# Second attention of a macaron block: the softmax sums over pre-added key halves, and a later order of the steps around them

## The reference

```
x = x + 0.5 * moe(norm(x));  x = x + attention0(norm(x));  x = x + 0.5 * moe(norm(x))
x = x + 0.5 * zones(norm(x)); x = x + attention1(norm(x));  x = x + 0.5 * zones(norm(x))
```

```
c_q, c_kv = h @ W_DQ + b_DQ, h @ W_DKV + b_DKV          # 32 features each
q = [c_q @ W_UQ + b_UQ, c_q @ W_QR + b_QR]              # 128 + 32 per head
k = [c_kv @ W_UK + b_UK, h @ W_KR + b_KR (all heads)]
attn = softmax(q k^T / sqrt(160))                       # 256 x 256 per head and batch
out = (attn @ (c_kv @ W_UV + b_UV)) @ W_O + b_O
```

## Time and profile before

| what | us |
|---|---|
| median of 3 runs | 1517.97 |
| lowest and highest | 1517.54, 1518.09 |
| the profiled execution | 1523.39 |
| its span | 1521.4 |
| TensorE busy | 1457.4 (96%) |
| VectorE busy | 1099.7 (72%) |
| ScalarE busy | 958.2 (63%) |
| GpSimd busy | 581.7 (38%) |

### The profile page before, as it was taken

One profiled execution on the slowest core, in us unless ns is written; L12 is line 12 of the kernel. 1 busy time (PEld: TensorE's weight loads), 2 busy tenths in 40 slices (PEclk: granted clock), 3 DMA queues, 4 the chain that ended last, 5 costly groups with the idle time before them and its releaser, 6 DMA issues.

```text
span 1521.4 us, 27946 instructions
## 1 busy us (share of the span) xinstructions
PE 1457.4 (96%) x9950; PEld 1186.2 (78%) x9950; DVE 1099.7 (72%) x2377; ACT 958.2 (63%) x1710; POOL 581.7 (38%) x551
## 2 busy tenths in 40 slices
PE   6999999889999999999999999999979999989998
PEld 6788888775666665688888877899967777769998
DVE  3766766688888888476667665577768888866765
ACT  6455555447777777655555554777736666668886
POOL 4466566510000000026666653677710111136664
PEclk9999999999999999999999996999999999999999
DMA  6000000000000000000000003000000000000000
GB/s 176 1 1 1 1 0 2 1 0 2 1 1 1 1 2 1 1 1 1 2 0 1 1 26 143 1 2 2 2 1 2 1 2 2 2 2 2 15 15 29
DMA packets 13320, 16.88 MB, mean 11 GB/s; under 512 B 768, under 2 KB 10496, under 8 KB 12928
## 3 DMA queue, kind: packets, MB, share of 16 engines
q1 hardware_dynamic: 13184, 15.11, 3.2%
HBM read 13.01 MB, written 2.10 MB: 10 GB/s over the span
## 4 chain that ended last, share of the span: by engine, by line
PE 84%; DVE 8%; ACT 4%; issue 2%; DMA 1%; POOL 0%; DVEq 0%; SPq 0%; POOLq 0%; ACTq 0%
PE PS L604 20%; PE PS L632 10%; PE PS L1748 9%; PE PS L1761 8%; PE PS L741 5%; PE PS L761 5%; PE PS L749 4%; PE PS L1118 2%; PE PS L718 2%; PE PS L1093 2%; PE PS L1122 2%; PE PS L170 2%; PE PS L1075 1%; PE PS L1103 1%; PE PS L1142 1%
## 5 line engine op out<-in xcount | busy, mean ns | idle before, releaser
L542 POOL TENSOR_TENSOR RR<-AR,RR 128x512 fp32r<-128x512 f32 x150 | 193.9, 1293 | 490.7 <-ACT RR L565 490.7
L579 ACT ACTIVATE AR<-PS 128x512 f32<-128x512 f32 x224 | 134.0, 598 | 197.2 <-PE PS L604 196.0
L521 DVE TENSOR_TENSOR AR<-AR,PS 128x512 f32<-128x512 f32 x224 | 153.8, 687 | 132.3 <-PE PS L604 132.2
L859 ACT ACTIVATE AR<-PS 128x512 f32<-128x512 f32 x256 | 152.3, 603 | 85.9 <-PE PS L749 85.2
L932 DVE TENSOR_REDUCE AR<-PS 128x2 f32<-128x512 f32 x256 | 172.3, 686 | 21.5 <-PE PS L741 20.8
L604 PE MATMUL PS<-XHI,WG 128*128 128x512 f32 x448 | 175.7, 392 | 0.0
L604 PE MATMUL PS<-XHI,WU 128*128 128x512 f32 x448 | 174.6, 390 | 0.2
L525 DVE TENSOR_TENSOR AR<-AR,PS 128x512 f32<-128x512 f32 x224 | 153.9, 687 | 7.9 <-POOL RR L542 0.3
L1748 PE MATMUL PS<-XHI,SL 128*128 128x256 f32 x576 | 133.7, 287 | 2.6 <-DVE XTR L1914 1.5
L1748 PE MATMUL PS<-XLO,SL 128*128 128x256 f32 x576 | 133.0, 286 | 1.5 <-DVE XTR L1914 1.3
L741 PE MATMUL PS<-XLO,XHI 128*128 128x512 f32 x256 | 129.5, 506 | 3.0 <-DVE AR L932 2.4
(11 more groups left out here) (299 smaller groups left out, 3489.4 us busy)
## 6 DMA issues: line engine op xcount, KB each, us to landing
X<-in_x SPq DMA_DIRECT2D x4, 512.0 KB, 6.6
RAWZ<-in_zone_up SPq DMA_DIRECT2D x8, 256.0 KB, 5.0
RAWZ<-in_zone_down SPq DMA_DIRECT2D x8, 256.0 KB, 5.6
out_x<-X SPq DMA_DIRECT2D x4, 512.0 KB, 3.2
AR<-in_w SPq DMA_DIRECT2D x1, 1792.0 KB, 11.7
XT<-in_w SPq DMA_DIRECT2D x1, 1608.0 KB, 8.8
XT<-in_sel SPq DMA_DIRECT2D x1, 896.0 KB, 6.8
SM<-in_small SPq DMA_DIRECT2D x1, 857.5 KB, 7.2
```

The lines of the kernel that those rows point to most:

```text
L521: v.tensor_tensor(PRD[:, m % 2, :], SIL[:, m % 2, :], bank(2 + m % 2), ALU.mult).then_inc(S.prod, 1)
L542: g.tensor_tensor(HL[k % 3], GAT[:, m % 2, :], HH[k % 3].bitcast(F32), ALU.subtract).then_inc(S.h_lo, 1)
L579: act.activation(SIL[:, m % 2, :], bank(m % 2), ACT.Silu).then_inc(S.silu, 1)
L859: act.activation(PT[:, g % 2, k, 2 * jp:2 * jp + 2, :], bank(2 + m % 2).rearrange("p (j q) -> p j q", j=2), ACT.Exp, scale=SC0).then_inc(S ...
```

## The change

GpSimd gets a new step `pairs(b, half)`: it adds the two key halves of a half batch's exponentials into a tile PAIR (128x1024, fp32, in the second half of RR). The product with ones moves out of `values` into `sums(b, g)`, which runs over PAIR with four matmuls instead of over both key halves with eight; the last half batch, (15, 1), still uses both halves. The slots change on TensorE, ScalarE and VectorE: sums, copies, turnings, `project_out`, `add`, `stats`, `normalise` and `normed` come one slot or more later. TensorE's `project_out` and first `turn` move past the end of the step, and so for the last batch into the next stage's beginning.

```diff
--- before.py
+++ after.py
@@ -176,7 +176,7 @@
         BOTH = ("stats_done dve_chain m_chain r_chain rstd_in xn tr xt kv qh qs v s_pe smax mm mt qs2 st_pe "
                 "exp av os ot ao aot_pe aot out x_new st_new zero xb")
         kinds = {"f0": FFN0, "f1": FFN1, "a0": BOTH + " k_chain kx q qx ks",
-                 "a1": "m_chain r_chain kv qh qs v s_pe smax mm mt qs2 st_pe exp av os ot ao aot_pe aot out x_new zero xb kl kp_pe kp_hi "
+                 "a1": "m_chain r_chain kv qh qs v s_pe smax mm mt qs2 st_pe exp pair av os ot ao aot_pe aot out x_new zero xb kl kp_pe kp_hi "
                        "kp_lo raw_in blank prep_pe prep_hi prep_lo prep_copy"}
 
 
@@ -1008,6 +1008,7 @@
         QH1 = XLO[:, 3072:3328]
         QS1 = [XLO[:, 3328 + u * SEQ:3328 + (u + 1) * SEQ] for u in range(3)]
         VA1 = SM[:, va_at:va_at + 256].rearrange("p (u k d) -> p u k d", u=4, k=2)
+        PAIR = RRF[:, 1024:2048].rearrange("p (j q) -> p j q", j=4)
         NS1 = NH1
         NQ1 = NH1 // 2
         LEAD1 = 3
@@ -1036,9 +1037,18 @@
                 xs = X[:, b * TPB:(b + 1) * TPB, :]
                 g.tensor_tensor(xs, xs, CBB.unsqueeze(1).to_broadcast([P, TPB, H]), ALU.add).then_inc(S.xb, 1)
 
+            def pairs(b, half):
+                g.wait_ge(S.exp, NS1 * b + 4 * half + 4)
+                wait(g, S.av, 2 * b + half)
+                g.tensor_tensor(PAIR, PT[:, half, 0, :, :], PT[:, half, 1, :, :], ALU.add).then_inc(S.pair, 1)
+
             for i in range(-1, NB):
+                if i >= 1:
+                    pairs(i - 1, 1)
                 if i >= 2:
                     next_power(g, n, i - 2)
+                if i >= 0:
+                    pairs(i, 0)
                 if i + 1 < NB:
                     bias(i + 1)
                 if i == NB - 2:
@@ -1117,10 +1127,18 @@
                     for j in range(4):
                         pe.matmul(o[32 * j:32 * j + 32, 0:SEQ], VA1[:, b % 4, k, :], PT[:, g, k, j, :],
                                   start=(k == 0), stop=(k == 1), skip_group_check=True)
-                for k in range(2):
+
+            def sums(b, g):
+                o = bank(6 + g)
+                if (b, g) == (NB - 1, 1):
+                    parts = [PT[:, g, k, :, :] for k in range(2)]
+                else:
+                    pe.wait_ge(S.pair, 2 * b + g + 1)
+                    parts = [PAIR]
+                for k, part in enumerate(parts):
                     for j in range(4):
-                        last = pe.matmul(o[32 * j:32 * j + 32, SEQ:2 * SEQ], ones[:, 0:32], PT[:, g, k, j, :],
-                                         start=(k == 0), stop=(k == 1), skip_group_check=True)
+                        last = pe.matmul(o[32 * j:32 * j + 32, SEQ:2 * SEQ], ones[:, 0:32], part[:, j, :],
+                                         start=(k == 0), stop=(k == len(parts) - 1), skip_group_check=True)
                 last.then_inc(S.av, 1)
 
             def turn(b, g):
@@ -1171,26 +1189,30 @@
                         early_route_pe(n + 1, m)
                     if m == 0 and far:
                         project(i + 2)
+                    if m == 0 and gone:
+                        project_out(i - 2)
+                    if m == 0 and done:
+                        turn(i - 1, 0)
                     if m == 1 and done:
                         values(i - 1, 1)
-                    if m == 3 and gone:
+                    if m == 2 and done:
+                        sums(i - 1, 1)
+                    if m == 4 and gone:
                         next_turn(i - 2)
-                    if m == 3 and done:
+                    if m == 4 and done:
                         turn(i - 1, 1)
                     if m == 5 and now:
                         values(i, 0)
-                    if m == 5 and done:
+                    if m == 6 and done:
                         back(i - 1)
+                    if m == 6 and now:
+                        sums(i, 0)
                     if m == 6 and next_:
                         maxima(i + 1)
-                    if m == 7 and now:
-                        turn(i, 0)
-                    if m == 7 and done:
-                        project_out(i - 1)
 
             for i in range(-2, NB):
                 step(i)
-            TAIL["pe"] = names(dict(values=values, turn=turn, back=back, project_out=project_out, next_turn=next_turn))
+            TAIL["pe"] = names(dict(values=values, sums=sums, turn=turn, back=back, project_out=project_out, next_turn=next_turn))
 
         def a1_act(n):
             S = ST[n]
@@ -1236,10 +1258,12 @@
             def step(i):
                 now, far, done, gone = (0 <= i + d < NB for d in (0, 2, -1, -2))
                 for m in range(NS1):
-                    if m == 2 and done:
+                    if m == 3 and done:
                         out_sums(i - 1, 1)
-                    if m == 6 and now:
+                    if m == 7 and now:
                         out_sums(i, 0)
+                    if m == 5 and gone:
+                        next_copy(i - 2)
                     if now:
                         exps(i, m)
                     if m == 0 and far:
@@ -1248,12 +1272,10 @@
                     if m == 2 and far:
                         head_keys(i + 2, 0)
                         head_keys(i + 2, 1)
-                    if m == 4 and gone:
-                        next_copy(i - 2)
                     if m == 4 and far:
                         head_keys(i + 2, 2)
                         head_keys(i + 2, 3)
-                    if m == 6 and done:
+                    if m == 7 and done:
                         turned(i - 1)
                     if i == NB - 2 and m in (1, 3, 5, 7):
                         early_high(n + 1, m // 2)
@@ -1343,22 +1365,23 @@
                     b, s = divmod(NS1 * (i + 1) + LEAD1 + m, NS1)
                     if m == 7 and next_:
                         shift(i + 1)
+                    if m == 1 and gone:
+                        add(i - 2)
                     if 0 <= b < NB:
                         smax(b, s)
-                    if m == 0 and done:
+                    if m == 1 and gone:
+                        stats(i - 2)
+                    if m == 1 and done:
                         normalise(i - 1, 0)
-                    if m == 0 and gone:
-                        add(i - 2)
-                        stats(i - 2)
                     if m == 1 and far:
                         low_inputs(i + 2)
                         vals(i + 2)
                         stacks(i + 2)
-                    if m == 1 and gone:
+                    if m == 3 and gone:
                         normed(i - 2)
                     if m == 4 and next_:
                         maxima(i + 1)
-                    if m == 4 and done:
+                    if m == 5 and done:
                         normalise(i - 1, 1)
                     if m == 3 and far:
                         head_keys(i + 2, 0)
@@ -1786,7 +1809,10 @@
 
             if resident:
                 A = TAIL["pe"]
+                A.project_out(NB - 2)
+                A.turn(NB - 1, 0)
                 A.values(NB - 1, 1)
+                A.sums(NB - 1, 1)
                 up(0)
                 A.turn(NB - 1, 1)
                 up(1)
```

## The result

The change makes the kernel slower: 1596.85 us median of 4 runs (1593.66 to 1597.44), against 1518.03 for the kernel before in the same session, a ratio of 1.0505 (95% interval 1.0485 to 1.0525). The profiled execution took 1597.35 us with a span of 1595.4, where that of before took 1523.39 with 1521.4. The forecast was 1535, with a range up to 1567.

A forecast was written before the change was run, and what follows sets the result against it. TensorE's columns bound the second attention, with VectorE's in-order queue able to take savings back. Twelve full batches at +1.2 us (14.4), first two -0.8, end +3.5: +17 on 1518, so 1535 us, range 1523 to 1567.

The forecast's parts named there:

- the likeliest case: Full batches wait on VectorE's queue in slots 2 and 4, period 15.7 us; 1527 to 1545 us, chance 0.62.
- VectorE comes first by 0.05 us, in every batch alike: Slot 3: the second normed starts at 9.03, GpSimd's first-half add at 9.08, so normed is not held.
- the layout: Computed schedule of one full batch from slot 0's scores, using measured intervals: period 15.7 us against 14.5.
- Rival one: GpSimd's add blocks VectorE's second normed about 2.4 us a batch, delaying slot 4; 1555 to 1568 us, chance 0.17.
- The waits: TensorE loses 0.92 us in slot 2 for vals and 1.29 in slot 4 for the first key stack, per batch.
- The saving, 0.86 from halving: Four fewer matmuls per sums' product save 0.43 us, 0.86 per batch; net 0.70 after switches between tile widths.
- The adds at no cost for GpSimd's own load: Two adds of 2.36 us per batch raise GpSimd to 6.4 busy us of 14.5, costing nothing in full batches.
- The end: Late GpSimd add for batch 14's second half, plus turning and project_out before the feed-forward: about +3.5 us.
- The first steps: First two batches, without an older batch's project_out in slot 0, keep part of the saving: about -0.8 us.
- Rival two: TensorE does not wait for VectorE's queue; batch 13.8 us, 0.7 less, about 1508 us; chance 0.09.

The follow-up runs named there:

- experiment 7: Kernel after with project_out, its copies, add and stats back in old slots, normed in slot 2, two key stacks before the maximum: 1515.86 us, ratio 0.9977.
- experiment 4: Kernel after plus twelve matmuls into a bank nobody reads, in slot 4 before the head keys: 1581.62 us, ratio 1.0404.
- experiment 1: Kernel after without GpSimd's adds, every sums' product over both key halves, the new slots kept: 1555.12 us, ratio 1.0237.
- experiment 3: Kernel after with each GpSimd add cut into four pieces of 128x256: 1557.33 us, ratio 1.0247.
- experiment 2: Kernel after with VectorE's normed in slot 2 instead of slot 3: 1543.50 us, ratio 1.0153.
- experiment 5: experiment 2 plus stats and first normalise moved behind low_inputs, vals and stacks in VectorE's slot 1: 1530.16 us, ratio 1.0067.
- experiment 11: experiment 7 without GpSimd adds, every sums' product over both key halves: 1522.03 us, ratio 1.0014.
- experiment 6: Kernel before plus GpSimd's two adds per batch (batches 0 to 14), results unread: 1522.35 us, ratio 1.0015.
- experiment 9: experiment 7 without GpSimd's last two adds; half batches (14, 1) and (15, 0) use the full product: 1510.12 us, ratio 0.9932.
- experiment 12: Kernel before with only VectorE's first and third key stacks moved ahead of the maximum of their slot: 1519.98 us, ratio 1.0001.

## Why the prediction was wrong

The direction held, and the likeliest case's waits in slots 2 and 4 are there, but with them the batch would be 16.4 us; the 3.8 us from there to 20.18 come from two other steps of the prediction, which failed.

**The step that failed: "VectorE comes first by 0.05 us, in every batch alike".** From slot 0 the layout had the second `normed` at 9.03 and the add at 9.08. Measured they stand at 1252.01 and 1252.06 less 1242.67, at 9.34 and 9.39: the margin of 0.05 was right to the hundredth (both hang on the same slot 3, so what the layout lacked before it moved them alike), and GpSimd still won: the prediction had put the hold on `normed` at nothing. The second `normed` is recorded 0.08 us before the first ends (1252.09); the add starts inside that overlap. What the margin had to be measured from is not the recorded start of the second instruction. Two other meetings in these traces narrow it. In the kernel after, in an earlier stage, the second of two such scalings is recorded 0.10 us ahead of an add that starts after the first has ended; it keeps its 0.33, and the add takes 2.46 us in place of 2.35:
```profile
923.02 0.33 DVE L1619 TENSOR_SCALAR XN<-X,LN 128x128 f32<-128x128 f32 x1
...
923.12 2.46 POOL L2026 TENSOR_TENSOR ZW<-RAWZ,ZW 128x1024 fp32r<-128x1024 f32 x1 [1.22 <-ACT ZW L1593]
```
In experiment 7 a scaling of 8x8 (0.22 us in the kernel before), its predecessor on VectorE over by then, is recorded 0.03 us ahead of an add and is held by it:
```profile
1341.27 2.40 DVE L1664 TENSOR_SCALAR AR<-AR 8x8 f32<-8x8 f32 x1
...
1341.30 2.35 POOL L1043 TENSOR_TENSOR RRF<-AR 128x1024 f32<-128x1024 f32 x1 [0.95 <-ACT AR L1241]
```
So a recorded lead of 0.03 or 0.05 us lost and one of 0.10 won; an earlier instruction of VectorE still under way is not needed for the loss. Where between them the order turns, and what decides it, no run shows. What is shown is that the meeting costs 2.1 to 2.2 us a batch at full clock (18.54 in experiment 4 against 16.38, which is experiment 1's 17.25 less the 0.87 of the full products; or 2.475 less 0.34), and that the hold lasts one GpSimd instruction (experiment 3). Rival one had the mechanism and a price of 2.4 a batch; its chance of 0.17 was far too small for a margin of 0.05 in a sum whose terms were off by more than that.

The Trainium skill ("SBUF — State Buffer", section "SBUF: two separate sides") says that whichever starts first, GpSimd or a VectorE instruction that uses the shared ports, gets them for the whole instruction. The length of the hold agrees (2.475 us beside an add of 2.34). Taken by the recorded starts, the order does not: there the loser started 0.05 us earlier.

**The term that was missing: the clock.** I priced TensorE's new waits by their length alone, with every row from a stage at 1.00. With waits of 0.8 and 3.4 us in each batch the granted clock came to 0.88 over the full batches, and TensorE's own work got longer: 1.64 us a batch (20.18 to 18.54), 18 us over the eleven. This is most of what rival one's 1565 lacked to the 1596.85; the layout below has another 8.

**The layout was 0.7 us short.** Without the hold of 2.475 less 0.34 the batch of experiment 4 is 18.54 less 2.14, 16.4, not 15.7 (experiment 2 is a further 0.5 lower, since `normed` no longer stands in front of the stack at all), and experiments 1 and 2 missed their forecasts by 0.75 and 0.66. The rows of the timeline after show where: `back` before the sums 0.53 (0.39 forecast, 1259.32 to 1259.85), `project_out` 0.98 (0.91), the signal from `vals` to TensorE 0.14 (0.04), head keys to sums 1.10 (1.04, with 0.10 for a restart where half of my own 0.29 for two is 0.15). From a slot's pair to the value product behind it I took 0.56; it is 0.73 in slot 5 (1257.01 to 1257.74). In slot 1 it is 0.64, which costs nothing, since TensorE waits for `vals` behind it. The five that count make 0.54 together, no one of them large, and the rest is steps of 0.03 or less. The weak terms were those carried over to other neighbours, as four transposes at two thirds of six.

**The other steps.** The waits stand where I put them: slot 2 for `vals` (0.78 of idle time, 0.92 forecast; moving what stood before `vals` gained 0.88, experiment 5) and slot 4 for the first key stack. The saving, 0.86 from halving: right (0.87, experiment 11); PE has 248 fewer records, 9702. The adds at no cost for GpSimd's own load: right (experiment 6). The end was mis-sized: +3.5 forecast, +9.6 measured. By TensorE's value products, 2.0 of it lie between (13, 0) and (14, 0), with one more hold on `normed`, 2.1 up to (15, 0), and 5.5 behind that. The add for (14, 1) does stand behind the last low part, as forecast. The add for (15, 0), to which I had given no cost, runs from 1425.42 to 1427.79 and holds a small scaling of the next stage's routing to its end (0.22 us in the kernel before), and behind that TensorE waits 2.79 us for a normalise; the clock was at 0.86 over the two steps. How the 5.5 divide between the hold and the clock is open. With the places of experiment 7 the step from (14, 0) to (15, 0) takes 14.84 us, and 10.61 without the two adds (experiment 9). GpSimd's and VectorE's timelines of the kernel after:
```profile
1419.91 1.27 POOL L1549 TENSOR_TENSOR XHI<-XF,XLO 128x512 fp32r<-128x512 f32 x1 [1.95 <-ACT XLO L1541]
1421.14 2.36 POOL L1043 TENSOR_TENSOR RRF<-AR 128x1024 f32<-128x1024 f32 x1
...
1425.82 1.99 DVE L1671 TENSOR_SCALAR AR<-AR 8x8 f32<-8x8 f32 x1
```
The first steps were no saving of 0.8 but a loss of 6.4, since hold and waits were at work there too.

**Where the full batch's time goes,** each difference between two kernels that ran:

| step | us a batch | from |
|---|---|---|
| kernel before | 14.50 | |
| kernel after | 20.18 | |
| clock | -1.64 | experiment 4, 18.54 |
| `normed` out of the add's way and out from before the key stack | -2.68 | experiment 2, 15.86 |
| statistics and normalise ahead of `vals` | -0.88 | experiment 5, 14.98 |
| the other places, and two key stacks ahead of the maximum | -1.15 | experiment 7, 13.83 |
| back to full products | +0.87 | experiment 11, 14.70 |

Of the 2.68 the hold is 2.1 to 2.2, the rest is `normed`'s place before the key stack.

Rival two had put the period at 13.8 and the time at 1508. Experiment 9 has 13.83 and 1510.12: the saving is there once VectorE's queue is not what TensorE waits for, and the slots of the change, with the meeting that they led to, were what gave it away. What stays open is how the 1.15 divides, between slots moved back and the stacks' new order (which alone gains nothing in the kernel before, experiment 12), and the small loss of the places in experiment 11 (0.2), which I ascribe to the value product and the sums standing apart without having tried it.

## What to carry to other kernels

Moving work off the bound engine is half of a change; the other half is what moves in the queue that feeds it. List for each instruction whom it delays there, and put what the bound engine waits for first. When two engines can hold each other, a computed margin smaller than the error of the layout is no margin: price both orders, or move one of the two a slot away. And a long wait of TensorE that comes back in every batch may cost more than its length: here one of 3.4 us took another 1.64 by the clock, where waits of 0.8 and 1.2 took none.

## What the runs showed of the hardware

- A VectorE instruction recorded 0.05 us before GpSimd's (behind another one without a pause) or 0.03 us before it (the one before it over) still lost to it: 2.475 us instead of 0.34, 2.40 instead of 0.22. One recorded 0.10 us before it won.
- What GpSimd's adds hold is not only the scalings from SBUF to SBUF: in experiment 7 the cast of 128x16 took 1.345 us (median), in the kernel before 0.174. The row maxima, which read PSUM, are not held (experiment 9, VectorE's timeline during an add of GpSimd from 1252.56 to 1254.95, the cast behind it held to the add's end):
```profile
1252.91 0.68 DVE L1321 TENSOR_REDUCE AR<-PS 128x2 f32<-128x512 f32 x1
1253.63 1.35 DVE L1330 CAST RR<-AR 128x16 fp32r<-128x16 f32 x1
```
- Matmuls whose result is dropped (2.84 us a batch) made the kernel after 15 us faster, with TensorE's granted clock at 1.00 in place of 0.88.
